# Cross-attention softmax on ScalarE from PSUM, and the first expert pair scaled by ScalarE

## The chip, the cores and the metric

One core of a Trainium2 chip runs one program. The metric is the device time in microseconds (us), the median of three runs. The engines are TensorE (PE, with its weight loads PEld), VectorE (DVE), ScalarE (ACT), GpSimd (POOL) and SyncE (SP), which issues the transfers. Each runs its own queue of instructions in order; semaphores tie them together. Matmul results land in PSUM banks; VectorE and ScalarE read them there and write to SBUF.

## What is computed

64 sequences of 256 tokens, 256 channels, in fp32. First a cross-attention block with a context of 77 rows and 8 heads of 64, then a block in which routing weights over 16 experts mix projections:

```python
x = x + xattn(layernorm(x), ctx)            # heads 8, width 64, context 77
    # q = x@Wq, k = ctx@Wk, v = ctx@Wv
    # softmax(q k^T * SCALE) v, then @Wo + bo         SCALE = 64 ** -0.5
x = x + ffn(layernorm(x))
    # rw = gating(x)                       weights over 16 experts, per token
    # q = sum_e rw[e] * (x @ q_proj[e]), likewise k and v   (64 columns each)
    # attn = causal softmax(q k^T / 8) v
    # out = sum_e (attn * rw[e]) @ o_proj[e]
```

## The kernel before, in words

A sequence has two tiles of 128 tokens. fp32 products are made of three products of a high and a low part (`_hi`, `_lo`, in a rounded format), by `product` (lines 371 to 375): so most PSUM results are copied by ScalarE into the high part and subtracted from it by VectorE into the low part.

The work of a sequence is cut into pieces with one function each on every engine that takes part: `a_...` is the cross-attention, `b_...` LayerNorm 2, routing and the expert projections, `c_...` the second attention and the output experts. Each engine runs `step(i)` for one sequence after the other: a list, written by hand, of pieces of sequence i+1 (`ahead`), i (`now`), i-1 (`before`) and i-2 (`earlier`). That list is the engine's order (TensorE lines 610 to 654, ScalarE 782 to 810, VectorE 1054 to 1105, GpSimd 1262 to 1279); a piece waits at its start for what it needs, and everything behind it in the same list waits with it.

PSUM has three rings of banks: `bank_a` (3), `bank_b` (3) and `bank_c` (2). Fill number f of a ring uses bank f modulo the ring's size, so TensorE may only start fill f when fill f-3 (in a and b) has been read. `ring_a` and `ring_b` (lines 380 to 393) wait for that. The fills that matter here: the four score blocks `a_s` 0 to 3 are fills 7 to 10 of ring a, the transposes `a_pT` 0 and 1 fills 11 and 12, `a_pv` 0 fill 13. So `a_s` 3 follows `a_s` 0 in the same bank, `a_pT` 0 and 1 follow `a_s` 1 and 2, and `a_pv` 0 follows `a_s` 3. The expert projections are `b_qkv` 0 to 15, two of the 16 experts for one token tile each; `b_qkv` j+3 follows `b_qkv` j in a bank of ring b. `b_qkv` 0 and 1 (the opening pair, one for each tile) also hold the routing logits.

A score block holds four heads for one token tile, 4 x 77 = 308 columns. VectorE takes the row maximum of each head from PSUM (line 923) and writes scores minus maximum to `probs` in SBUF (line 925), which frees the bank. ScalarE takes the exponential in place, one instruction of 308 columns, with the factor SCALE (line 719). VectorE sums the exponentials of two blocks (line 930) and takes the reciprocal (line 933), and GpSimd multiplies (line 1247). TensorE then transposes `probs` (line 485).

The routing weights `rw` come last from a chain: sum (line 977) and reciprocal (line 979) on VectorE, product on GpSimd (line 1224). VectorE scales the two experts of `b_qkv` 0 and 1 by `rw` into the accumulators `acc` (line 993) and adds the other seven pairs to them (line 996). Of the second attention, `c_pT` (split on ScalarE at line 740 and on VectorE at line 1002), `c_pv` (its result copied by ScalarE at line 768), and `c_mix` 0 to 3 (VectorE line 1037, ScalarE 772, GpSimd 1252) lie near the change. ScalarE's softmax there (`c_exp`, line 754) already uses a bias from SBUF and an accumulator.

Of the kernel before, what the change touches and what calls it, by code (L numbers as in the profile page):

```python
# [34 lines left out]
def xattn_moe_kernel(nc, x, ctx_in, Wq, Wk, Wv, Wo, bo, sim_matrix, gates, q_proj, k_proj, v_proj, o_proj, out, rw_dram):  # L35
# [35 lines left out]
    def b_at(n, fill):  # L71
        return B_FILLS * n + fill + 1
# [2 lines left out]
        return C_FILLS * n + fill + 1  # L75

    def a_read(n, fill):
        assert fill % A_FILLS != A_K
        return (A_FILLS - 1) * n + fill + (1 if fill < A_K else 0)

    def b_read(n, fill):
        return (B_QKV + 2 * NT * EP) * n + (fill + 1 if fill < B_QKV else 2 * fill)

    C_READ = {C_QK: 0, C_S: 2, C_PT: 3, C_Y: 4}

# [19 lines left out]
    with es:  # L105
# [6 lines left out]
        def sem(name):  # L112
            return es.enter_context(nc.semaphore(name))
# [256 lines left out]
        def _(pe):  # L370
# [9 lines left out]
            def ring_a(n, fill):  # L380
                if fill - A_BANKS == A_K:
                    pe.wait_ge(k_ready, at(1, n, 0))
                elif fill >= A_BANKS:
                    pe.wait_ge(a_evac, a_read(n, fill - A_BANKS))
                elif not (known(n) and n == 0):
                    pe.wait_ge(a_evac, a_read(n - 1, fill - A_BANKS + A_FILLS))

            def ring_b(n, fill):
                if not (known(n) and n == 0 and fill < B_BANKS):
                    if fill >= B_BANKS:  # L390
# [212 lines left out]
            def step(i):  # L603
                ahead, now, before, earlier = i + 1, i, i - 1, i - 2

                def do(n, fn, *k):
                    if on(n):
                        fn(n, *k)

                do(before, b_qkv, 6)  # L610
                do(before, b_qkv, 7)
                do(earlier, c_y, 0)
                do(before, b_qkv, 8)
                do(earlier, c_y, 1)
# [24 lines left out]
                do(now, b_qkv, 0)  # L639
                do(now, b_qkv, 1)  # L640
                do(ahead, a_kT)
                do(before, c_s)
                do(ahead, a_q, 0)
                do(ahead, a_q, 1)
                do(now, b_qkv, 2)
                do(ahead, a_s, 0)
                do(before, c_pT)
                do(ahead, a_s, 1)
                do(ahead, a_s, 2)
                do(ahead, a_s, 3)  # L650
                do(before, c_pv)
                do(now, b_qkv, 3)
                do(now, b_qkv, 4)
                do(now, b_qkv, 5)
# [10 lines left out]
        def _(act):  # L665
# [6 lines left out]
            def split_weights(k):  # L672
                hi = PIECES[k][1]
                act.wait_ge(wt_in[k % SLOTS], 16 * loads_before(k))
                nc.scalar.activation(hi, stage[k % SLOTS][:, 0:hi.shape[1]], copy).then_inc(wt_hi, 1)

            for k in range(EARLY):
                split_weights(k)
# [36 lines left out]

            def a_exp(n, j):
                half, t = j // 2, j % 2
                act.wait_ge(a_evac, a_read(n, A_S + j))
                nc.scalar.activation(probs[:, t, half * HB:(half + 1) * HB, :], probs[:, t, half * HB:(half + 1) * HB, :],  # L719
                                     ACT.Exp, scale=SCALE).then_inc(p_exp, 1)  # L720

            def a_pT(n, j):
                t = j % 2
# [10 lines left out]
            def b_exp(n):  # L734
                act.wait_ge(g_ready, at(1, n, 0))
                nc.scalar.activation(w[:, :, :], g[:, :, :], ACT.Exp).then_inc(e_ready, 1)

            def c_part(n, fill, dst, src):
                act.wait_ge(c_fill, c_at(n, fill))
# [34 lines left out]
            def step(i):  # L774
                ahead, now, before, earlier = i + 1, i, i - 1, i - 2

                def do(n, fn, *k):
                    if on(n):
                        fn(n, *k)
                        later(split_weights, fn.__name__.replace("exp", "s"), n, *k)  # L780
# [22 lines left out]
                do(ahead, a_q, 1)  # L803
                do(now, b_exp)
                do(before, c_pT)
                do(before, c_pv)
                do(before, c_mix, 0)
                do(ahead, a_exp, 0)
                do(before, c_mix, 1)
                do(before, c_mix, 2)  # L810

# [9 lines left out]
        def _(dve):  # L821
# [12 lines left out]
            def split_weights(k):  # L834
                dve.wait_ge(wt_hi, k + 1)
                for lo, hi, rows, cols in PIECES[k][2]:
                    last = V.tensor_tensor(lo, stage[k % SLOTS][rows, cols], hi.bitcast(F32), ALU.subtract)
                last.then_inc(wt_ready, 1)

            def ln_a(k, n, src):  # L840
# [76 lines left out]
                last.then_inc(a_evac, 1)  # L917

            def a_s(n, j):
                half, t = j // 2, j % 2  # L920
# [60 lines left out]
            def b_qkv(n, j):  # L981
                fill, ep, t = B_QKV + j, j // NT, j % NT
                dve.wait_ge(b_fill, b_at(n, fill))
                if j == 0:
                    dve.wait_ge(rw_ready, at(1, n, 0))
                if ep == 0 and not (known(n) and n == 0):
                    dve.wait_ge(qkv_ready, at(NT, n - 1, t))
                for k in range(2):
                    e = 2 * ep + k
                    lo = (E if ep == 0 else 0) + k * QKV  # L990
                    src = bank_b(fill)[:, lo:lo + QKV]
                    if ep == 0:
                        V.tensor_scalar(acc[:, t, k, :], src, rw[:, t, e:e + 1], None, ALU.mult).then_inc(b_evac, 1)  # L993
                    else:
                        dve.wait_ge(b_evac, b_read(n, fill - NT) - 1 + k)
                        V.scalar_tensor_tensor(acc[:, t, k, :], src, rw[:, t, e:e + 1], acc[:, t, k, :],  # L996
                                               ALU.mult, ALU.add).then_inc(b_evac, 1)


            def c_part(n, fill, which, pair, src):  # L1000
# [45 lines left out]
            def step(i):  # L1046
# [96 lines left out]
        def _(pool):  # L1143
# [98 lines left out]
                G.tensor_tensor(v2[1][:, :, :, :], v_in, v2[0].bitcast(F32)[:, :, :, :], ALU.subtract).then_inc(v2_ready, 1)  # L1242

            def a_p(n, half):
                pool.wait_ge(p_sum_ready, at(4, n, 2 * half + 1))
# [72 lines left out]
```

## Time and profile before

| | us |
|---|---|
| median of three runs (2802.65 to 2807.08) | 2802.98 |
| the profiled run's own time | 2805.71 |
| its span, from first to last instruction | 2803.8 |
| TensorE matmuls busy | 2702.4 (96%) |
| VectorE busy | 2439.1 (87%) |
| ScalarE busy | 1020.0 (36%) |
| GpSimd busy | 1190.0 (42%) |
| mean granted TensorE clock | 0.991 of full |

The busy shares say which engine is nearly full. They don't say where it waits: for that there are the table of waits (who waited for whom, summed), the timeline (instructions with their start in us from the span's start, their duration, and idle time before them in brackets) and the busy time in a window. In the steady part the steps repeat with the same times, so one step can be read for all.

### The profile page before, as it was taken

To read this page: it belongs to the slowest core of one execution; us is meant where nothing else is said; L and a number is where in the kernel's file an instruction comes from. 1 tells how busy PE (TensorE), PEld (TensorE's weight loads), DVE (VectorE), ACT (ScalarE), POOL (GpSimd) and SP (SyncE) were. 2 spreads that over 40 slices of the span, in tenths; PEclk is the share of its full clock that TensorE was granted. 3 is DMA by queue.
4 is the path that set the end of the run, shared out by engine and by line. 5 is a ranking of instruction groups with operands and counts; after the bars stand their busy time and mean duration, and the time that the engine had idled before them with its cause. 6 is when DMAs were issued, how large, how long until landed. Compare 5 with 4: busy or idle time off the path is not lost.

```text
span 2803.8 us, 64494 instructions
## 1 busy us (share of the span) xinstructions
PE 2702.4 (96%) x19012; PEld 2581.8 (92%) x19012; DVE 2439.1 (87%) x6755; ACT 1020.0 (36%) x2448; POOL 1190.0 (42%) x1739
## 2 busy tenths in 40 slices
PE   5999999999999999999999999999999999999996
PEld 4999999999999999999999999999999999999996
DVE  6898888888888888988988889888889889888884
ACT  3343333333333333433333333333334334333331
POOL 1343443444444434434434434444344344344343
PEclk8999999999999999999999999999999999999998
DMA  4111111111111111111111111111111111111111
GB/s 103 29 45 44 32 44 35 40 44 28 44 48 28 44 44 31 44 44 31 44 39 36 44 30 41 48 28 44 44 31 44 44 31 44 43 32 44 35 36 39
DMA packets 131435, 113.58 MB, mean 41 GB/s; under 512 B 24720, under 2 KB 130640, under 8 KB 131408
## 3 DMA queue, kind: packets, MB, share of 16 engines
q1 hardware_dynamic: 131408, 113.23, 16.5%
q8 instruction: 15, 0.25, 0.0%
q14 instruction: 12, 0.10, 0.0%
HBM read 95.38 MB, written 17.83 MB: 40 GB/s over the span
## 4 chain that ended last, share of the span: by engine, by line
PE 73%; DVE 12%; issue 9%; ACT 4%; POOL 1%; DVEq 1%; POOLq 0%; DMA 0%; ACTq 0%; SPq 0%
PE bank_b L373 9%; PE bank_b L374 8%; PE bank_a L375 8%; PE bank_b L375 8%; PE bank_a L374 8%; PE bank_a L373 8%; PE bank_c L373 4%; PE bank_c L375 4%; PE bank_c L374 4%; PE bank_a L485 4%; DVE acc L996 3%; DVE acc L993 2%; DVE mix L1037 1%; PE bank_a L445 1%; DVE s_max L923 1%
## 5 line engine op out<-in xcount | busy, mean ns | idle before, releaser
L373 PE MATMUL bank_b<-wqkv_hi,x2T_lo 128*128 128x384 f32 (+1 forms) x2048 | 726.4, 355 | 34.3 <-DVE acc L996 33.7
L374 PE MATMUL bank_b<-wqkv_lo,x2T_hi 128*128 128x384 f32 (+1 forms) x2048 | 693.5, 339 | 0.0
L375 PE MATMUL bank_b<-wqkv_hi,x2T_hi 128*128 128x384 f32 (+1 forms) x2048 | 688.8, 336 | 0.0
L996 DVE SCALAR_TENSOR_TENSOR acc<-bank_b,rw,acc 128x192 f32<-128x192 f32 x1792 | 641.6, 407 | 5.3 <-PE bank_b L375 2.9
L1252 POOL TENSOR_TENSOR mixs_lo<-mix,mixs_hi 128x512 fp32r<-128x512 f32 x256 | 379.9, 1514 | 153.7 <-ACT mixs_hi L772 153.7
L373 PEld LDWEIGHTS bank_b<-wqkv_hi,x2T_lo 128*128 128x128 f32 x2048 | 385.8, 188 | 57.5 <-DVE acc L996 53.6
L374 PEld LDWEIGHTS bank_b<-wqkv_lo,x2T_hi 128*128 128x128 f32 x2048 | 386.2, 189 | 0.0
L375 PEld LDWEIGHTS bank_b<-wqkv_hi,x2T_hi 128*128 128x128 f32 x2048 | 385.1, 188 | 0.0
L1174 POOL TENSOR_TENSOR pow_out<-pow_in,expo 128x2 f32<-128x2 f32 (+1 forms) x128 | 111.7, 873 | 596.4 <-DVE pow_in L853 509.3
L373 PE MATMUL bank_c<-wo_hi,mixs_lo 128*128 128x256 f32 x1024 | 293.9, 287 | 3.7 <-POOL mixs_lo L1252 3.7
L375 PE MATMUL bank_c<-wo_hi,mixs_hi 128*128 128x256 f32 x1024 | 288.0, 281 | 0.0
L374 PE MATMUL bank_c<-wo_lo,mixs_hi 128*128 128x256 f32 x1024 | 287.9, 281 | 0.0
L1037 DVE TENSOR_TENSOR mix<-rw_all,aT 128x512 f32<-128x512 f32 x256 | 243.0, 970 | 2.3 <-ACT aT L768 2.1
L772 ACT ACTIVATE mixs_hi<-mix 128x512 fp32r<-128x512 f32 x256 | 160.6, 628 | 205.6 <-DVE mix L1037 205.6
L1247 POOL TENSOR_TENSOR probs<-probs,p_sum 128x616 f32<-128x616 f32 x128 | 155.9, 1218 | 175.7 <-DVE p_sum L933 175.7
L682 ACT ACTIVATE aT_hi<-bank_a 128x512 fp32r<-128x512 f32 x128 | 76.4, 597 | 412.8 <-PE bank_a L375 412.8
L373 PEld LDWEIGHTS bank_c<-wo_hi,mixs_lo 128*128 128x128 f32 x1024 | 193.6, 189 | 4.1 <-issue 3.8
L374 PEld LDWEIGHTS bank_c<-wo_lo,mixs_hi 128*128 128x128 f32 x1024 | 194.4, 190 | 0.0
L375 PEld LDWEIGHTS bank_c<-wo_hi,mixs_hi 128*128 128x128 f32 x1024 | 193.9, 189 | 0.0
L889 DVE TENSOR_TENSOR aT_lo<-bank_a,aT_hi 128x512 fp32r<-128x512 f32 x128 | 88.5, 692 | 116.7 <-ACT aT_hi L682 116.7
L719 ACT ACTIVATE probs<-probs 128x308 f32<-128x308 f32 x256 | 117.2, 458 | 185.4 <-DVE probs L925 185.4
L889 DVE TENSOR_TENSOR pT_lo<-bank_a,pT_hi 77x512 fp32r<-77x512 f32 x256 | 162.9, 676 | 0.2 <-ACT pT_hi L682 0.2
(196 smaller groups left out, 6991.1 us busy)
## 6 DMA issues: line engine op xcount, KB each, us to landing
rw_all<-rw_dram SPq DMA_DIRECT2D x128, 512.0 KB, 5.7
xt<-in_x_dram SPq DMA_DIRECT2D x64, 256.0 KB, 2.7
out_dram<-mix SPq DMA_DIRECT2D x64, 256.0 KB, 2.2
ct<-in_ctx_dram SPq DMA_DIRECT2D x64, 57.8 KB
ct<-in_ctx_dram SPq DMA_DIRECT2D x64, 19.2 KB
mix<-in_L_ffn_o_proj_dram SPq DMA_DIRECT2D x2, 512.0 KB, 4.2
rw_dram<-rwT SPq DMA_DIRECT2D x64, 16.0 KB, 1.4
x_tiles<-in_L_xattn_Wq_dram SPq DMA_DIRECT2D x1, 512.0 KB, 6.9
```

Source lines behind the costliest of these rows:

```text
L373: nc.tensor.matmul(dst, lhs[1], rhs[0], start=start, stop=False)
L374: nc.tensor.matmul(dst, lhs[0], rhs[1], start=False, stop=False)
L375: return nc.tensor.matmul(dst, lhs[0], rhs[0], start=False, stop=stop)
L485: last = nc.tensor.transpose(bank_a(fill)[0:NC, k * P:(k + 1) * P], probs[:, t, half * HB + k, :], ident[:, :])
L719: nc.scalar.activation(probs[:, t, half * HB:(half + 1) * HB, :], probs[:, t, half * HB:(half + 1) * HB, :], ACT.Exp, scale=SCALE).then_in ...
L772: nc.scalar.activation(mixs[0][:, 2 * j:2 * j + 2, :], mix[:, 2 * j:2 * j + 2, :], copy).then_inc(mix_hi, 1)
L889: V.tensor_tensor(pair[1], src, pair[0].bitcast(F32), ALU.subtract).then_inc(a_evac, 1)
L996: V.scalar_tensor_tensor(acc[:, t, k, :], src, rw[:, t, e:e + 1], acc[:, t, k, :], ALU.mult, ALU.add).then_inc(b_evac, 1)
L1037: V.tensor_tensor(mix[:, 2 * j:2 * j + 2, :], rw_all[:, 2 * j:2 * j + 2, :], aT2[:, :].unsqueeze(1).to_broadcast([P, 2, T]), ALU.mult).the ...
L1174: G.tensor_tensor(dst, src, expo[:, 0:m], ALU.pow).then_inc(ln_pow[k], 1)
L1247: G.tensor_tensor(part, part, p_sum[:, half, 1, :, :].unsqueeze(3).to_broadcast([P, NT, HB, NC]), ALU.mult).then_inc(p_ready, 1)
L1252: G.tensor_tensor(mixs[1][:, 2 * j:2 * j + 2, :], mix[:, 2 * j:2 * j + 2, :], mixs[0].bitcast(F32)[:, 2 * j:2 * j + 2, :], ALU.subtract).t ...
```

## The change

The exponentials of the cross-attention are taken from PSUM by ScalarE: for each head an instruction of 77 columns, with the negated maximum as bias and the row's sum as accumulator output. VectorE's subtraction and its sum go; it keeps the maximum (negated in the same instruction) and the reciprocal, which now waits for the exponentials. SCALE moves into Wq when the weights are split at the start. A score bank is now free when its exponentials are done: the fills that follow (`a_s` 3, `a_pT` 0 and 1, `a_pv` 0) wait for `p_exp`.

The opening expert pair is scaled by ScalarE (`b_first`, two copies of 192 columns with a scale from SBUF for each tile), signalled by `acc_first`; `b_qkv` 3 and 4 on TensorE and `b_qkv` 2 and 3 on VectorE wait for it. In ScalarE's order the two `b_first` come after `c_pT`, and `a_exp` 0 now comes after them and ahead of `c_pv` and `c_mix` 0. In TensorE's order `c_pv` moves ahead of `a_s` 3.

```diff
@@ TensorE, ring_a and ring_b @@
+                elif A_S <= fill - A_BANKS < A_S + 2 * NT:
+                    pe.wait_ge(p_exp, at(2 * NT, n, fill - A_BANKS - A_S))
...
+                    if B_QKV <= fill - B_BANKS < B_QKV + NT:
+                        pe.wait_ge(acc_first, at(NT, n, fill - B_BANKS - B_QKV))
@@ TensorE, step @@
                 do(ahead, a_s, 2)
+                do(before, c_pv)
                 do(ahead, a_s, 3)
-                do(before, c_pv)
@@ ScalarE @@
-                nc.scalar.activation(hi, stage[k % SLOTS][:, 0:hi.shape[1]], copy).then_inc(wt_hi, 1)
+                nc.scalar.activation(hi, stage[k % SLOTS][:, 0:hi.shape[1]], copy,
+                                     scale=SCALE if k == W_Q else 1.0).then_inc(wt_hi, 1)
...
             def a_exp(n, j):
                 half, t = j // 2, j % 2
-                act.wait_ge(a_evac, a_read(n, A_S + j))
-                nc.scalar.activation(probs[:, t, half * HB:(half + 1) * HB, :], probs[:, t, half * HB:(half + 1) * HB, :],
-                                     ACT.Exp, scale=SCALE).then_inc(p_exp, 1)
+                act.wait_ge(s_max_ready, at(2 * NT, n, j))
+                for k in range(HB):
+                    last = nc.scalar.activation(probs[:, t, half * HB + k, :], bank_a(A_S + j)[:, k * NCE:k * NCE + NC], ACT.Exp,
+                                                bias=s_max[:, j, k:k + 1], accum_out=p_sum[:, half, 0, t, k:k + 1])
+                last.then_inc(p_exp, 1)
...
+            def b_first(n, t):
+                act.wait_ge(rw_ready, at(1, n, 0))
+                act.wait_ge(b_fill, b_at(n, B_QKV + t))
+                if known(n) and n == 0:
+                    act.wait_ge(sim_step, 5)
+                else:
+                    act.wait_ge(qkv_ready, at(NT, n - 1, t))
+                for e in range(2):
+                    last = nc.scalar.activation(acc[:, t, e, :], bank_b(B_QKV + t)[:, E + e * QKV:E + (e + 1) * QKV], copy,
+                                                scale=rw[:, t, e:e + 1])
+                last.then_inc(acc_first, 1)
@@ ScalarE, step @@
                 do(before, c_pT)
+                do(now, b_first, 0)
+                do(now, b_first, 1)
+                do(ahead, a_exp, 0)
                 do(before, c_pv)
                 do(before, c_mix, 0)
-                do(ahead, a_exp, 0)
@@ VectorE @@
             def a_s(n, j):
...
-                V.tensor_reduce(s_max[:, j, :], src, AX.X, ALU.max).then_inc(s_max_ready, 1)
-                dve.wait_ge(s_max_ready, at(2 * NT, n, j))
-                V.tensor_tensor(probs[:, t, half * HB:(half + 1) * HB, :], src,
-                                s_max[:, j, :].unsqueeze(2).to_broadcast([P, HB, NC]), ALU.subtract).then_inc(a_evac, 1)
+                V.tensor_reduce(s_max[:, j, :], src, AX.X, ALU.max, negate=True).then_inc(s_max_ready, 1)
             def a_psum(n, half):
                 dve.wait_ge(p_exp, at(2 * NT, n, 2 * half + 1))
-                V.tensor_reduce(p_sum[:, half, 0, :, :], probs[:, :, half * HB:(half + 1) * HB, :], AX.X,
-                                ALU.add).then_inc(p_sum_ready, 1)
-                dve.wait_ge(p_sum_ready, at(4, n, 2 * half))
+                if not (known(n) and n == 0):
+                    dve.wait_ge(p_ready, at(2, n - 1, half))
                 V.reciprocal(p_sum[:, half, 1, :, :], p_sum[:, half, 0, :, :]).then_inc(p_sum_ready, 1)
...
-                    if ep == 0:
-                        V.tensor_scalar(acc[:, t, k, :], src, rw[:, t, e:e + 1], None, ALU.mult).then_inc(b_evac, 1)
+                    if ep == 1:
+                        dve.wait_ge(acc_first, at(NT, n, t))
@@ VectorE, step @@
                 do(before, c_pT)
-                do(now, b_qkv, 0)
-                do(now, b_qkv, 1)
                 do(now, b_qkv, 2)
```

Besides, VectorE's split of Wq multiplies by SCALE, the counts in `a_read` and `b_read` follow, and GpSimd's `a_p` waits for the new count of the reciprocals.

## Rows read from the trace of the kernel before

**Rows 1.** The page: busy time; chain that ended last; line 719's group.
```profile
PE 2702.4 (96%) x19012; PEld 2581.8 (92%) x19012; DVE 2439.1 (87%) x6755; ACT 1020.0 (36%) x2448; POOL 1190.0 (42%) x1739
...
PE 73%; DVE 12%; issue 9%; ACT 4%; POOL 1%; DVEq 1%; POOLq 0%; DMA 0%; ACTq 0%; SPq 0%
...
L719 ACT ACTIVATE probs<-probs 128x308 f32<-128x308 f32 x256 | 117.2, 458 | 185.4 <-DVE probs L925 185.4
```

**Rows 2.** Windows, one step: length; busy PE, PEld, DVE, ACT, POOL; clock, DMA.
```profile
1340.73:1383.32 42.59, 41.88 (x298) 40.10 (x297) 37.78 (x106) 15.72 (x38) 18.54 (x27) 1.00 0.16 39
```

**Rows 3.** Waits of TensorE's weight loads, whole run: us in total, times, longest.
```profile
PEld bank_b L373 <- DVE acc L996: 53.6, 62, 0.9
PEld bank_c L541 <- POOL late_tiles L1232: 26.7, 60, 0.5
PEld bank_c L549 <- DVE k_stack L1007: 18.3, 59, 0.3
```

**Rows 4.** Timeline of TensorE at `b_qkv` 7: start, duration, instruction, idle before.
```profile
1353.48 0.33 PE L375 MATMUL bank_b<-wqkv_hi,x2T_hi 128*128 128x384 f32 x1
1354.37 0.44 PE L373 MATMUL bank_b<-wqkv_hi,x2T_lo 128*128 128x384 f32 x1 [0.55 <-DVE acc L996]
1354.65 0.34 PE L374 MATMUL bank_b<-wqkv_lo,x2T_hi 128*128 128x384 f32 x1
```

**Rows 5.** Timeline of VectorE in the same step, `a_s` 0 to `b_qkv` 4.
```profile
1346.63 0.48 DVE L923 TENSOR_REDUCE s_max<-bank_a 128x4 f32<-128x308 f32 x1 [0.26 <-PE bank_a L375]
1347.14 0.48 DVE L925 TENSOR_TENSOR probs<-bank_a,s_max 128x308 f32<-128x308 f32 x1
1347.54 0.17 DVE L977 TENSOR_REDUCE w_sum<-w 128x2 f32<-128x32 f32 x1
1347.75 0.17 DVE L979 RECIPROCAL w_sum<-w_sum 128x2 f32<-128x2 f32 x1
...
1348.42 1.39 DVE L993 TENSOR_SCALAR acc<-bank_b,rw 128x192 f32<-128x192 f32 x4
1349.73 0.73 DVE L996 SCALAR_TENSOR_TENSOR acc<-bank_b,rw,acc 128x192 f32<-128x192 f32 x2
1350.38 1.28 DVE L1037 TENSOR_TENSOR mix<-rw_all,aT 128x512 f32<-128x512 f32 x2
...
1352.23 1.42 DVE L1037 TENSOR_TENSOR mix<-rw_all,aT 128x512 f32<-128x512 f32 x1
1353.58 0.73 DVE L996 SCALAR_TENSOR_TENSOR acc<-bank_b,rw,acc 128x192 f32<-128x192 f32 x2
```

**Rows 6.** Groups by line, VectorE, one step: count, busy us, mean ns.
```profile
L930 DVE TENSOR_REDUCE p_sum<-probs 128x8 f32<-128x616 f32 x2 | 1.6, 782 | 0.0
```

**Rows 7.** Timeline of ScalarE: the second attention's softmax, then `c_pT`.
```profile
1344.01 0.39 ACT L754 ACTIVATE late_tiles<-late_tiles,m 128x128 f32<-128x128 f32 x1
1344.30 0.19 ACT L754 ACTIVATION_READ_ACCUMULATOR late_tiles<-late_tiles,m 128x1 f32 x1
1344.39 0.50 ACT L754 ACTIVATE late_tiles<-late_tiles,m 128x256 f32<-128x256 f32 x1
...
1346.97 0.49 ACT L740 ACTIVATE p2T_hi<-bank_c 128x384 fp32r<-128x384 f32 x1 [1.30 <-PE bank_c L557]
```

**Rows 8.** Timeline of ScalarE: copies of 77 columns from PSUM.
```profile
1375.39 0.24 ACT L692 ACTIVATE cT_hi<-bank_a 128x77 fp32r<-128x77 f32 x1 [5.56 <-PE bank_a L424]
1375.52 0.22 ACT L693 ACTIVATE cT_hi<-bank_a 64x77 fp32r<-64x77 f32 x1
```

**Rows 9.** Timeline of GpSimd: the routing weights.
```profile
1348.08 0.24 POOL L1224 TENSOR_TENSOR rw<-w,w_sum 128x32 f32<-128x32 f32 x1 [1.10 <-DVE w_sum L979]
```

**Rows 10.** Timeline of TensorE: first matmuls of `a_s` 3, `c_pv` and `b_qkv` 3.
```profile
1348.07 0.28 PE L373 MATMUL bank_a<-kT_hi,qT_lo 128*128 128x156 f32 x1
...
1348.74 0.32 PE L373 MATMUL bank_c<-p2T_hi,v_lo 128*128 128x256 f32 x1
...
1349.41 0.39 PE L373 MATMUL bank_b<-wqkv_hi,x2T_lo 128*128 128x384 f32 x1
```

More of the change, by code:

```diff
@@ L77, in a_read @@
     def a_read(n, fill):
-        assert fill % A_FILLS != A_K
-        return (A_FILLS - 1) * n + fill + (1 if fill < A_K else 0)
+        assert fill != A_K and not A_S <= fill < A_S + 2 * NT
+        return (A_FILLS - 1 - 2 * NT) * n + fill + (1 if fill < A_K else 0) - (2 * NT if fill > A_S else 0)
     def b_read(n, fill):
-        return (B_QKV + 2 * NT * EP) * n + (fill + 1 if fill < B_QKV else 2 * fill)
+        assert not B_QKV <= fill < B_QKV + NT
+        return (B_QKV + 2 * NT * (EP - 1)) * n + (fill + 1 if fill < B_QKV else 2 * (fill - NT))
     C_READ = {C_QK: 0, C_S: 2, C_PT: 3, C_Y: 4}
@@ L229, in xattn_moe_kernel @@
         pad_done = sem("pad_done")
+        acc_first = sem("acc_first")
         passed = sem("passed")
@@ L389, in ring_b @@
                 if not (known(n) and n == 0 and fill < B_BANKS):
-                    if fill >= B_BANKS:
+                    if B_QKV <= fill - B_BANKS < B_QKV + NT:
+                        pe.wait_ge(acc_first, at(NT, n, fill - B_BANKS - B_QKV))
+                    elif fill >= B_BANKS:
                         pe.wait_ge(b_evac, b_read(n, fill - B_BANKS))
@@ L836, in split_weights @@
                 for lo, hi, rows, cols in PIECES[k][2]:
-                    last = V.tensor_tensor(lo, stage[k % SLOTS][rows, cols], hi.bitcast(F32), ALU.subtract)
+                    if k == W_Q:
+                        last = V.scalar_tensor_tensor(lo, stage[k % SLOTS][rows, cols], SCALE, hi.bitcast(F32),
+                                                      ALU.mult, ALU.subtract)
+                    else:
+                        last = V.tensor_tensor(lo, stage[k % SLOTS][rows, cols], hi.bitcast(F32), ALU.subtract)
                 last.then_inc(wt_ready, 1)
@@ L919, in a_s @@
             def a_s(n, j):
-                half, t = j // 2, j % 2
                 src = bank_a(A_S + j)[:, 0:HB * NCE].rearrange("p (a b) -> p a b", a=HB)[:, :, 0:NC]
                 dve.wait_ge(a_fill, a_at(n, A_S + j))
-                V.tensor_reduce(s_max[:, j, :], src, AX.X, ALU.max).then_inc(s_max_ready, 1)
-                dve.wait_ge(s_max_ready, at(2 * NT, n, j))
-                V.tensor_tensor(probs[:, t, half * HB:(half + 1) * HB, :], src,
-                                s_max[:, j, :].unsqueeze(2).to_broadcast([P, HB, NC]), ALU.subtract).then_inc(a_evac, 1)
+                V.tensor_reduce(s_max[:, j, :], src, AX.X, ALU.max, negate=True).then_inc(s_max_ready, 1)
             def a_psum(n, half):
                 dve.wait_ge(p_exp, at(2 * NT, n, 2 * half + 1))
-                V.tensor_reduce(p_sum[:, half, 0, :, :], probs[:, :, half * HB:(half + 1) * HB, :], AX.X,
-                                ALU.add).then_inc(p_sum_ready, 1)
-                dve.wait_ge(p_sum_ready, at(4, n, 2 * half))
+                if not (known(n) and n == 0):
+                    dve.wait_ge(p_ready, at(2, n - 1, half))
                 V.reciprocal(p_sum[:, half, 1, :, :], p_sum[:, half, 0, :, :]).then_inc(p_sum_ready, 1)
@@ L983, in b_qkv @@
                 dve.wait_ge(b_fill, b_at(n, fill))
[L984 to L987, printed above, removed]
                 for k in range(2):
                     e = 2 * ep + k
-                    lo = (E if ep == 0 else 0) + k * QKV
-                    src = bank_b(fill)[:, lo:lo + QKV]
-                    if ep == 0:
-                        V.tensor_scalar(acc[:, t, k, :], src, rw[:, t, e:e + 1], None, ALU.mult).then_inc(b_evac, 1)
+                    src = bank_b(fill)[:, k * QKV:(k + 1) * QKV]
+                    if ep == 1:
+                        dve.wait_ge(acc_first, at(NT, n, t))
                     else:
                         dve.wait_ge(b_evac, b_read(n, fill - NT) - 1 + k)
-                        V.scalar_tensor_tensor(acc[:, t, k, :], src, rw[:, t, e:e + 1], acc[:, t, k, :],
-                                               ALU.mult, ALU.add).then_inc(b_evac, 1)
+                    V.scalar_tensor_tensor(acc[:, t, k, :], src, rw[:, t, e:e + 1], acc[:, t, k, :],
+                                           ALU.mult, ALU.add).then_inc(b_evac, 1)
             def c_part(n, fill, which, pair, src):
@@ L1244, in a_p @@
             def a_p(n, half):
-                pool.wait_ge(p_sum_ready, at(4, n, 2 * half + 1))
+                pool.wait_ge(p_sum_ready, at(2, n, half))
                 part = probs[:, :, half * HB:(half + 1) * HB, :]
```

## The prediction

> **What bounds the kernel now.** I read the page first: TensorE is busy 96% of the span, VectorE 87%, ScalarE 36%, and TensorE holds 73% of the chain that ended last [rows 1]. VectorE's 12% of that chain shows that it sometimes hands TensorE its work late. The profiled run took 2805.71 us (span 2803.8), 2.7 us above the median of the three times, 2802.98; my sum starts at 2805.71, and I take 2.7 off at its end.
>
> The kernel repeats one step for each of 64 sequences. A stretch of one step lasts 42.59 us, with 41.88 us of matmuls, 37.78 us of VectorE and 15.72 us of ScalarE [rows 2]. So a lighter VectorE as such gives nothing; only the places where TensorE stands still count. The table of waits names three that come back in nearly every step [rows 3]: the weight load of an expert projection waits for VectorE's accumulation at line 996 (53.6 us, 62 times), the transposes of query and key wait for GpSimd's sum (26.7 us, 60 times), and the scores of the second attention wait for `k_stack` (18.3 us, 59 times).
>
> The first is the one that the change is near. In the timeline the matmuls of `b_qkv` 6 run 0.17 to 0.18 us apart; the next one, the first of `b_qkv` 7, should start at 1353.65, starts at 1354.37, and the second follows 0.28 later instead of 0.175. The loss is 0.72 + 0.10 = 0.82 us a step [rows 4]. Its cause is the bank of `b_qkv` 4, which VectorE reads only from 1353.58 on, since it is behind: from 1346.63 it works without a gap [rows 5].
>
> **VectorE, what is removed.** In each step four subtractions at line 925 (0.48 us each), four scalings at line 993 (1.39 us together) [rows 5] and two sums at line 930 (0.782 us each) [rows 6] go: 1.9 + 1.4 + 1.6 = 4.9 us of 37.78. Before the stalling read lie one subtraction, 0.50 us from start to start, and the scalings, 1.31 us (1348.42 to 1349.73) [rows 5]. That is 1.8 us ahead of a delay of 0.82, so by itself the stall at `b_qkv` 7 goes: minus 0.82 us in 62 steps, minus 51 us. The other two stalls stay: the path from the output projection over LayerNorm, `b_qkv` 15 and GpSimd's sum, and the one over ScalarE's four copies into `k_stack`, hold nothing that is removed. Negating the maximum costs nothing (the same reduction); scaling Wq's low part happens once, beside the start's DMAs, within 1 us either way. The reciprocal now waits for the exponentials instead of a sum; its old partner is gone.
>
> **ScalarE, what is added.** Of the exponentials, one of 308 columns (0.458 us) [rows 1] becomes four of 77, each with a read of the accumulator behind it. The nearest rows are those of the second attention's softmax [rows 7]: with a bias from SBUF and an accumulator the 128-column one takes 0.39, its read begins 0.29 after it and the next exponential 0.09 after that. The 256-column one takes 0.50, so a column costs about 0.8 ns and 51 columns fewer take off 0.04: 0.35 for 77 columns, a read 0.25 after it, and a pair each 0.34. Four pairs to the end of the last read (0.19) are 3 x 0.34 + 0.25 + 0.19 = 1.46 us. These rows read SBUF where the new ones read PSUM, so I keep both ends: 1.23 (a pair at 0.28, as if most of the read were hidden), and 2.16 if exponential (0.35) and read (0.19) don't overlap at all. ScalarE gets about 4 x 1.0 = 4 us a step more, plus the scalings; of 42.59 it now uses 15.7, so it doesn't become the bound by load.
>
> The opening pair's scalings are four copies of 192 columns from PSUM with a scale from SBUF. A plain copy of 77 columns from PSUM takes 0.24, and the next starts 0.13 after it, so 0.1 overlaps [rows 8]; with 0.8 ns a column 192 take 0.33 and start 0.23 apart. The exponential with a bias from SBUF and an accumulator is 0.11 longer than a plain copy of 128 columns would be (0.39 against 0.28). If the operand from SBUF is the reason, the scalings take 0.44 and start 0.34 apart. I take 0.34, since the row with such an operand is the nearest; 0.23 and 0.44 (no overlap) are the ends. The rows don't say whether the 0.11 belongs to the operand or to the accumulator. The Trainium skill does ("ScalarE: Activation LUTs", section "What ACT_TABLE_LOAD costs"): a per-partition pointer operand adds about 93 ns to an ACTIVATE and neighbours overlap by about the same; by its formula the four would be an estimated 4 x 0.346 = 1.38 us against my 1.36, where without that rule the low end, 0.92, would be as good.
>
> **The new wait, and who stands behind it.** Score block `a_s` 3 uses the bank of `a_s` 0. Until now it waited for VectorE's subtraction, over at 1347.62, and its matmuls ran from 1348.07: no stall. Now it waits for ScalarE's exponentials of block 0, and those are queued behind the two `b_first`, which wait for the routing weights. I follow it in the times of this step:
> - VectorE's maximum starts at 1346.63. Without the subtraction the sum of weights starts at 1347.04 instead of 1347.54, its reciprocal at 1347.25 instead of 1347.75, and GpSimd's `rw`, at 1348.08 now, 0.50 earlier, at 1347.58 [rows 5, 9].
> - The first user of `rw` starts 0.34 after it (1348.42 now) [rows 5, 9], so `b_first` starts at 1347.92. ScalarE is free by then (its copy of p2T ends at 1347.46) [rows 7].
> - Four scalings, 1.36: 1349.28. Four exponentials, 1.46: 1350.74. A weight load follows its release by 0.06 (accumulation over at 1354.31, matmul at 1354.37) [rows 4, 5]: 1350.80.
> - TensorE has work until then from the second attention's `c_pv`, which the change puts ahead of `a_s` 3. It would start at 1348.07 and be done after 0.67 (1348.74 to 1349.41 now) [rows 10]: 1348.74. VectorE's c_pT part is then ready at about 1348.05, just in time.
>
> So TensorE stands 1350.80 - 1348.74 = 2.06 us, and 0.05 for the slow first matmul: 2.11 us in each of 63 steps (all sequences but the first), plus 133 us.
>
> **What is queued behind it.** On TensorE the `b_qkv` 3 to 7; on ScalarE `c_pv`, then VectorE's `c_mix` and GpSimd's four `mixs_lo`. All start from the same event, so they move together. From the release of `a_s` 3, `b_qkv` 7 is due after 0.7 + 4 x 1.05 = 4.9 us (a projection is six matmuls by 0.175). VectorE's read of `b_qkv` 4 ends 4.6 to 4.8 after it: two `c_mix` end at about 1.6 (0.4 of ScalarE's copy and 1.28), `b_qkv` 3 can be read from 1.9 on and takes 0.65, then 1.35 for a `c_mix` beside GpSimd (1352.23 to 1353.58) and 0.73 [rows 5]. The cover is only 0.1 to 0.3 us; if it is gone, up to 0.3 us a step comes back (19 us). Further on blocks 1 to 3 have 1.46 each where 0.46 was; the transposes of `a_pT` and `a_pv` 0 keep by the same bookkeeping some 0.5 to 0.7 us of cover.
>
> **Sum.** 2805.7 + 133 - 51 = 2888 in the profiled run's terms, 2885 against the median. With the low ends of both ScalarE costs (0.92 + 1.23 instead of 2.82) the wait is 1.44 and the sum 63 x 0.67 = 42 us less, 2843; without overlap (1.76 + 2.16) it is 3.21 and the sum 69 more, 2954. Start and end of the run, some 80 us outside the steady steps, I leave as they are, within 5 us.
>
> **Rivals.**
> - *Slower still: ScalarE's chain becomes a second wait.* Small instructions don't overlap; `a_s` 3 costs 3.2 us, and the three later blocks are 0.7 us longer each, 2.1 us against some 0.7 of cover before `a_pv` 0, which costs another 1.4 a step. That is 2954 to 3040. Against it: the read of the accumulator overlaps both its neighbours by 0.1 [rows 7]. Chance 12%.
> - *The stall at `b_qkv` 7 survives in part,* because `c_mix` now starts after the exponentials. 0.3 us a step: 2904. For it: the cover of 0.1 to 0.3. Chance 13%.
> - *Faster: ScalarE's leg is short.* From the release of `rw` to the last exponential I have 2.82 us. If it is below 1.5 the new wait is smaller than the 0.82 that goes. At 1.3 the wait is 0.54 + 0.05, the step 0.23 shorter, 2789 us. It would need the scalings 0.15 and the exponentials 0.18 apart; the only pair so close is the 77-column copy at 0.13, without accumulator [rows 8]. Chance 6%.
> - *About even,* a leg near 1.5: 3%.
>
> **How the numbers follow.** The forecast (2843 to 2920) has 66%, the surviving stall 13%, the second wait 12%, even 3%, faster 6%. I name 2885. The range is 2835 to 2945: it leaves out the two last and most of the second wait. A measurement tells about 0.2% from no change. Faster 6%, within 0.2% 3%, slower 91%.
>
> **What would show it.** In the changed profile: a wait of the weight load at line 373 in bank_a for ScalarE's `probs`, about 2 us, 63 times; none, or under 0.3 us, of `b_qkv` 7 for VectorE; VectorE's busy time near 2439 - 64 x 4.9 = 2125 us; ScalarE's near 1020 + 64 x 5.4 = 1366; the other two waits as now; pairs of exponential and read 0.34 apart; scalings 0.34 apart; the step 43.9 us. I am wrong if ScalarE's leg is well under 2.4 us, or if a wait that I don't list, before `a_pT` or `a_pv` 0, appears.

## The result and the profile after

The changed kernel is slower: 2949.39 us, median of four runs (2947.88 to 2949.59), against 2803.93 for the kernel before in the same comparison. The ratio is 1.0516, with a 95% interval from 1.0498 to 1.0534. I had named 2885 us with 2945 as the upper end. The direction was right, the size was not: 64 of the 145 us were missing from the sum.

The page of the kernel after, busy time, chain and the group of the new exponentials (line 727; every row has the line numbers of its own kernel, so line 375 here is line 373 of the kernel before):

```profile
PE 2776.1 (94%) x19012; PEld 2668.4 (91%) x19012; DVE 2122.6 (72%) x6115; ACT 1313.3 (45%) x4496; POOL 1162.7 (39%) x1739
...
PE 82%; ACT 9%; DVE 4%; issue 3%; POOL 1%; ACTq 0%; DMA 0%; POOLq 0%; DVEq 0%; SPq 0%
...
L727 ACT ACTIVATE probs<-bank_a,s_max 128x77 f32<-128x77 f32 x1024 | 317.2, 335 | 57.5 <-DVE s_max L949 57.5
```

VectorE is 316 us less busy than in [rows 1], and ScalarE's share of the chain went from 4% to 9%. But TensorE has 74 us more of busy time with the same 19012 matmuls: some of them ran longer. The same can be seen in the mean granted clock, 0.962 against 0.991 before.

The waits of TensorE's weight loads, whole run:

```profile
PEld bank_a L375 <- ACT probs L727: 113.2, 64, 2.7
PEld bank_c L547 <- POOL late_tiles L1247: 26.9, 60, 0.5
PEld bank_c L555 <- DVE k_stack L1024: 19.1, 59, 0.3
```

The first line is the new wait of `a_s` 3, 113.2 / 64 = 1.77 us in the mean. The wait for VectorE's accumulation that headed [rows 3] (53.6 us) is gone, and the other two are as they were.

What stands behind the new wait is in TensorE's timeline: the end of `c_pv`, the first matmuls of `a_s` 3, and `b_qkv` 3 to 5.

```profile
1328.36 0.28 PE L377 MATMUL bank_c<-p2T_hi,v_hi 128*128 128x128 f32 x1
1330.27 0.34 PE L375 MATMUL bank_a<-kT_hi,qT_lo 128*128 128x156 f32 x1 [1.63 <-ACT probs L727]
1330.45 0.28 PE L376 MATMUL bank_a<-kT_lo,qT_hi 128*128 128x156 f32 x1
...
1331.22 0.52 PE L376 MATMUL bank_b<-wqkv_lo,x2T_hi 128*128 128x384 f32 x1
1331.54 0.52 PE L377 MATMUL bank_b<-wqkv_hi,x2T_hi 128*128 128x384 f32 x1
...
1334.69 0.34 PE L375 MATMUL bank_b<-wqkv_hi,x2T_lo 128*128 128x384 f32 x1
1334.87 0.34 PE L376 MATMUL bank_b<-wqkv_lo,x2T_hi 128*128 128x384 f32 x1
```

TensorE stood from the end of `c_pv` to 1330.27. One us after it resumed, the projections are 0.32 us apart instead of 0.175. Eleven of them take 3.47 us (1331.22 to 1334.69) instead of 1.93: 1.55 us lost. The windows of these stretches (columns as in [rows 2]; the clock is the third number from the end) show the clock:

```profile
1328.00:1330.20 2.20, 0.64 (x6) 0.50 (x5) 0.74 (x2) 2.20 (x13) 0.69 (x1) 1.00 0.12 13
1330.20:1332.00 1.80, 1.73 (x10) 1.73 (x11) 1.29 (x2) 0.97 (x4) 0.00 (x0) 0.78 0.39 129
1332.00:1334.00 2.00, 2.00 (x8) 2.00 (x7) 0.94 (x3) 0.55 (x1) 1.97 (x2) 0.50 0.00 0
1334.00:1336.00 2.00, 2.00 (x11) 2.00 (x11) 2.00 (x4) 0.63 (x1) 0.71 (x2) 0.84 0.00 0
1336.00:1338.00 2.00, 2.00 (x14) 2.00 (x13) 1.38 (x4) 1.62 (x8) 2.00 (x2) 1.00 0.00 0
```

The granted clock is full up to the stand, falls to 0.50 (1.2 of 2.4 GHz) behind it and is back at 1.00 by 1336; 0.78 and 0.84 are windows in which it changes. By the Trainium skill ("TensorE: Matmul & The Clock Gate", section "What's actually happening") the clock has two states, full and half, and how busy TensorE has been lately decides between them. The windows agree with the two states, 1.00 and 0.50; whether the stand is the reason, the experiments have to show.

Not every step has it. At 611.77 `a_s` 3 stood for the same time, and the projections behind it run at full pace:

```profile
611.77 0.34 PE L375 MATMUL bank_a<-kT_hi,qT_lo 128*128 128x156 f32 x1 [1.63 <-ACT probs L727]
...
612.90 0.33 PE L377 MATMUL bank_b<-wqkv_hi,x2T_hi 128*128 128x384 f32 x1
613.07 0.33 PE L375 MATMUL bank_b<-wqkv_hi,x2T_lo 128*128 128x384 f32 x1
```

The windows from one start of `a_s` 3 to the next tell three kinds of step apart (the last row is a stretch behind the start at 744.27):

```profile
611.77:655.41 43.64, 41.83 (x297) 40.22 (x297) 33.06 (x95) 20.31 (x71) 18.45 (x27) 1.00 0.15 38
655.41:700.61 45.20, 43.38 (x297) 41.77 (x297) 32.38 (x95) 20.29 (x71) 17.94 (x27) 0.96 0.14 37
744.27:790.96 46.69, 44.91 (x298) 43.30 (x298) 33.01 (x95) 20.30 (x71) 17.64 (x27) 0.93 0.14 36
...
744.20:750.80 6.60, 6.53 (x22) 6.53 (x23) 3.54 (x8) 2.16 (x5) 3.35 (x3) 0.50 0.10 35
```

Of the 49 steps that start between 400 and 2600 us, 17 are of the first kind (43.64 us, full clock), 24 of the second (45.21 us, one fall of 3.4 us) and 8 of the third (46.70 us, a fall of 6.8 us). So two steps in three have a fall, and the falls cost (24 x 1.57 + 8 x 3.06) / 49 = 1.27 us a step.

The account of a step without a fall: the stand costs 1.80 us (from 1328.47, where `a_s` 3 would have followed, to 1330.27) and 0.07 for the slow first matmul, and the old stall's 0.82 is gone. That makes 1.05 us more, and 43.64 is 1.05 above the 42.59 of [rows 2]. Over the whole run, start and end included, the spans differ by (2946.1 - 2803.8) / 63 = 2.26 us a step, which leaves 1.21 us for the clock.

That the stand makes the clock fall was theory (A) for the experiments. Its rival (B) was that the projections behind `a_s` 3 are slow because ScalarE, VectorE and GpSimd start on the same event and use the memories beside them. The steps at full pace, such as the one from 611.77, have the same work beside them and already speak against it. A third question was which half of the change, or which place in an order, makes the stand.

### The profile page after: what moved, and what is told of

It is laid out like the page before. It is cut to its first block, busy times and chain, and to the rows that moved or that the text cites. A ratio compares the mean times of both kernels' runs of the same rounds, so it can differ in the third digit from the quotient of the medians.

```text
span 2946.1 us, 65793 instructions
## 1 busy us (share of the span) xinstructions
PE 2776.1 (94%) x19012; PEld 2668.4 (91%) x19012; DVE 2122.6 (72%) x6115; ACT 1313.3 (45%) x4496; POOL 1162.7 (39%) x1739
## 4 chain that ended last, share of the span: by engine, by line
PE 82%; ACT 9%; DVE 4%; issue 3%; POOL 1%; ACTq 0%; DMA 0%; POOLq 0%; DVEq 0%; SPq 0%
PE bank_b L375 12%; PE bank_b L376 11%; PE bank_b L377 11%; PE bank_a L375 9%; PE bank_a L377 8%; PE bank_a L376 8%; PE bank_c L375 4%; PE bank_c L377 4%; PE bank_c L376 4%; PE bank_a L491 4%; ACT probs L727 3%; ACT acc L755 2%; PE bank_a L451 1%; DVE s_max L949 1%; PE bank_c L555 1%
## 5 line engine op out<-in xcount | busy, mean ns | idle before, releaser
L376 PE MATMUL bank_b<-wqkv_lo,x2T_hi 128*128 128x384 f32 (+1 forms) x2048 | 716.7, 350 | 0.0
L377 PE MATMUL bank_b<-wqkv_hi,x2T_hi 128*128 128x384 f32 (+1 forms) x2048 | 711.7, 348 | 0.0
L1267 POOL TENSOR_TENSOR mixs_lo<-mix,mixs_hi 128x512 fp32r<-128x512 f32 x256 | 357.1, 1419 | 286.7 <-ACT mixs_hi L793 286.7
L375 PEld LDWEIGHTS bank_b<-wqkv_hi,x2T_lo 128*128 128x128 f32 x2048 | 408.5, 199 | 0.2
L376 PEld LDWEIGHTS bank_b<-wqkv_lo,x2T_hi 128*128 128x128 f32 x2048 | 405.6, 198 | 0.0
L727 ACT ACTIVATE probs<-bank_a,s_max 128x77 f32<-128x77 f32 x1024 | 317.2, 335 | 57.5 <-DVE s_max L949 57.5
L1054 DVE TENSOR_TENSOR mix<-rw_all,aT 128x512 f32<-128x512 f32 x256 | 198.2, 796 | 87.9 <-ACT aT L789 87.9
L375 PE MATMUL bank_a<-kT_hi,qT_lo 128*128 128x156 f32 x512 | 153.8, 300 | 104.5 <-ACT probs L727 104.2
L727 ACT ACTIVATION_READ_ACCUMULATOR probs<-bank_a,s_max 128x1 f32 x1024 | 222.7, 217 | 0.0
L375 PEld LDWEIGHTS bank_a<-kT_hi,qT_lo 128*128 128x128 f32 x512 | 104.5, 204 | 113.7 <-ACT probs L727 113.2
```

The lines of the kernel that those rows point to most:

```text
L375: nc.tensor.matmul(dst, lhs[1], rhs[0], start=start, stop=False)
L376: nc.tensor.matmul(dst, lhs[0], rhs[1], start=False, stop=False)
L377: return nc.tensor.matmul(dst, lhs[0], rhs[0], start=False, stop=stop)
L727: last = nc.scalar.activation(probs[:, t, half * HB + k, :], bank_a(A_S + j)[:, k * NCE:k * NCE + NC], ACT.Exp, bias=s_max[:, j, k:k + 1], ...
L1054: V.tensor_tensor(mix[:, 2 * j:2 * j + 2, :], rw_all[:, 2 * j:2 * j + 2, :], aT2[:, :].unsqueeze(1).to_broadcast([P, 2, T]), ALU.mult).the ...
L1267: G.tensor_tensor(mixs[1][:, 2 * j:2 * j + 2, :], mix[:, 2 * j:2 * j + 2, :], mixs[0].bitcast(F32)[:, 2 * j:2 * j + 2, :], ALU.subtract).t ...
```

## The experiments

Each is compared with the kernel before, timed beside it (medians 2804.98 to 2806.03 us).

**Filling the stand with matmuls that nobody reads.**

```diff
+            def filler(n):
+                for k in range(12):
+                    nc.tensor.matmul(bank_c(C_PT)[:, 0:C], wo[0][:, 0, 0:P], wo[0][:, 0, :],
+                                     start=True, stop=True)
...
                 do(before, c_pv)
+                do(before, filler)
                 do(ahead, a_s, 3)
```

> The changed kernel with 12 extra matmuls of 256 columns (their result is never read) between c_pv and a_s 3, in the time in which TensorE waits for the exponentials of block 0. Theory A (the clock): the wait of about 1.8 us in each step makes the granted clock fall to half for some us behind it, and this costs about 1.2 us a step on average; twelve matmuls by 0.12 us fill 1.44 us of the wait, the clock stays full, a_s 3 starts when it did: 2949 - 63 x 1.2 = about 2872 us. Theory B (the matmuls behind the wait are slow since ScalarE, VectorE and GpSimd use the memories at the same time): no change, 2949 us, and those matmuls stay 0.32 us apart.

Measured: 2873.96 us, ratio 1.0245 (1.0228 to 1.0262). More work and 75 us less time. In three fences: its waits in a stretch of 2200 us of the steady part (the one used for all waits below), its timeline, and the window of that stretch:

```profile
PEld bank_a L375 <- ACT probs L733: 17.7, 50, 0.4
```

```profile
1338.75 1.64 PE L568 MATMUL bank_c<-wo_hi 128*128 128x256 f32 x12
1340.54 0.34 PE L375 MATMUL bank_a<-kT_hi,qT_lo 128*128 128x156 f32 x1
1340.71 0.28 PE L376 MATMUL bank_a<-kT_lo,qT_hi 128*128 128x156 f32 x1
```

```profile
400.00:2600.00 2200.00, 2182.83 (x15567) 2097.92 (x15567) 1667.60 (x4800) 1021.74 (x3518) 927.78 (x1361) 1.00 0.16 38
```

`a_s` 3 waits for the same exponentials and starts no earlier: 1340.54 is 2.53 us after `c_pv`'s first matmul at 1338.01, and 1375.48 is 2.53 after 1372.95 in the kernel after. Only the clock differs, 1.00 in the window where the kernel after has 0.97, and ScalarE and the others do the same work beside the projections. Theory B falls. Over the whole run the clock costs (2946.1 - 2871.7) / 63 = 1.18 us a step.

**A shorter filler: 5 matmuls instead of 12.**

```diff
-                for k in range(12):
+                for k in range(5):
```

> The changed kernel with 5 extra matmuls instead of the 12 of the filler run: TensorE stands idle for about 1.2 us instead of 1.8 (without filler) or 0.4 (with 12). The start of a_s 3 isn't moved. If the clock only falls after a stand as long as 1.8 us, this is 2874 us, as with 12; if 1.2 us is already too long, it is near 2949.

Measured: 2872.82 us, ratio 1.0239 (1.0222 to 1.0256), the same as with 12. TensorE now stands for a good microsecond in each step (waits, then timeline),

```profile
PEld bank_a L375 <- ACT probs L733: 59.3, 50, 1.2
```

```profile
1338.53 0.81 PE L568 MATMUL bank_c<-wo_hi 128*128 128x256 f32 x5
1340.31 0.34 PE L375 MATMUL bank_a<-kT_hi,qT_lo 128*128 128x156 f32 x1 [0.97 <-ACT probs L733]
```

and pays nothing for it in clock: all 50 steps between 400 and 2600 us last 43.6 us, as the steps without a fall do in the kernel after. In this kernel a stand of 1.2 us is free of it and one of 1.8 is not.

**Real work in the stand: `b_qkv` 3 ahead of `a_s` 3.**

```diff
                 do(before, c_pv)
-                do(ahead, a_s, 3)
                 do(now, b_qkv, 3)
+                do(ahead, a_s, 3)
                 do(now, b_qkv, 4)
```

> The changed kernel with b_qkv 3 ahead of a_s 3 in TensorE's order: 1.05 us of real work in the wait, so 0.8 us of it is left, as long as the stall of the kernel before. Theory A (the clock): the wait is 1.05 shorter and the clock stays full, 2949 - 63 x (1.05 + 1.2) = about 2807 us. Theory B (contention): 2949 - 66 = 2883 us.

Measured: 2836.02 us, ratio 1.011 (1.0093 to 1.0126): 113 us less than the kernel after, far more than the 66 of theory B, but 29 us above what A had expected. The waits in the same 2200 us say why:

```profile
PEld bank_a L375 <- ACT probs L727: 42.8, 51, 0.8
PEld bank_b L375 <- DVE acc L1013: 27.7, 51, 0.6
```

The stand of `a_s` 3 is down to 0.84 us, as expected, and the mean clock is 0.99. But the stall at a projection that waits for VectorE is back with 0.54 us: TensorE reaches it 1.05 us earlier, VectorE doesn't, since its `c_mix` still starts from ScalarE's copy of `c_pv`. In 62 steps that is 33 us; the difference to the expectation is 29.

**The exponentials of block 0 ahead of the scalings on ScalarE.**

```diff
-                do(now, b_first, 0)
-                do(now, b_first, 1)
                 do(ahead, a_exp, 0)
+                do(now, b_first, 0)
+                do(now, b_first, 1)
                 do(before, c_pv)
```

> The changed kernel with a_exp 0 ahead of the two b_first in ScalarE's order. The exponentials of block 0 need only VectorE's maximum, over 0.7 us before rw, and take 1.2 us: they end before c_pv does, a_s 3 doesn't wait and the clock stays full. The stall at b_qkv 7 is gone too if VectorE keeps ahead. Theory A: 2804 - 51 = about 2753 us. Rival: the scalings come 1.2 us later and with them c_pv's copy and c_mix, so part of the stall at b_qkv 7 comes back (0.3 us a step), 2770 us; if the order of the two doesn't matter, 2949.

Measured: 2797.21 us, ratio 0.9969 (0.9958 to 0.9981). The wait of `a_s` 3 is gone and with it all of the loss: the same instructions as in the kernel after, in another order, are 152 us faster. But it is 44 us above the expectation. Again there is a row of waits for VectorE, and VectorE's timeline says why:

```profile
PEld bank_b L375 <- DVE acc L1013: 35.9, 52, 0.7
...
1348.10 0.74 DVE L1013 SCALAR_TENSOR_TENSOR acc<-bank_b,rw,acc 128x192 f32<-128x192 f32 x2 [1.37 <-ACT acc L755]
```

0.69 us a step at the projections, in a kernel in which VectorE has 4.9 us less to do. It stands 1.37 us ahead of `b_qkv` 2 for the scalings, which are now behind the exponentials on ScalarE, and from there to its read of `b_qkv` 4 it works almost without a gap.

**ScalarE's copy of `c_pv` between the scalings,** to see whether the copy holds `b_qkv` 7 (against the order of the last experiment).

```diff
                 do(ahead, a_exp, 0)
                 do(now, b_first, 0)
-                do(now, b_first, 1)
                 do(before, c_pv)
+                do(now, b_first, 1)
```

> Both halves of the change, with another order on ScalarE: a_exp 0, b_first 0, the copy of c_pv, b_first 1. In the run with only a_exp 0 put ahead (2797 us) a stall of 0.7 us a step at b_qkv 7 stayed. If it stays because c_mix 0 waits for c_pv's copy, which stands behind both scalings, the copy now comes 0.6 us earlier, c_mix and with it b_qkv 4 too, and the stall falls to about 0.1: 2797 - 63 x 0.6 = 2760 us. Rival (VectorE's load or the late accumulators hold b_qkv 7, not the copy): within 5 us of 2797.

Measured: 2778.7 us, ratio 0.9909 (0.9892 to 0.9925). The stall falls, but only from 0.69 to 0.44 us:

```profile
PEld bank_b L375 <- DVE acc L1013: 23.1, 52, 0.5
```

The median went down by 18.5 us, (0.69 - 0.44) x 63 = 16 of them here. The rival (within 5 us of 2797) is refuted and the copy is part of the cause; my 0.6 us was too much. VectorE still stands 1.36 us for the scalings ahead of `b_qkv` 2, by the trace; no run tests what would take that wait away.

**Each half of the change alone.** First the exponentials, with the scalings back on VectorE:

```diff
# from the kernel after
-                do(now, b_first, 0)
-                do(now, b_first, 1)
                 do(ahead, a_exp, 0)
...
# VectorE
                 do(before, c_pT)
+                do(now, b_qkv, 0)
+                do(now, b_qkv, 1)
                 do(now, b_qkv, 2)
```

> Only the softmax half of the change: the exponentials on ScalarE from PSUM, the opening pair's scalings back on VectorE at their old place, the rest as in the changed kernel (c_pv ahead of a_s 3). Nothing stands before a_exp 0 on ScalarE, so a_s 3 waits for nothing or 0.1 us. VectorE reaches b_qkv 4 0.5 us earlier than before the change, since a subtraction is gone from that stretch; the stall there falls from 0.8 to 0.3 us: 2804 - 63 x 0.5 = about 2772 us. Rival (the exponentials themselves cost the time, wherever the scalings are): 2850 or more.

Measured: 2771.99 us, ratio 0.9878 (0.9861 to 0.9894), as expected to the microsecond. TensorE waits for VectorE's accumulation 0.29 us a step:

```profile
PEld bank_b L374 <- DVE acc L1013: 14.9, 52, 0.3
```

Then the scalings alone, from the kernel before:

```diff
# ScalarE, from the kernel before
                 do(before, c_pT)
+                do(now, b_first, 0)
+                do(now, b_first, 1)
                 do(before, c_pv)
# VectorE
-                do(now, b_qkv, 0)
-                do(now, b_qkv, 1)
                 do(now, b_qkv, 2)
```

> The kernel before with only the scaling half of the change: the opening pair scaled by ScalarE, ahead of c_pv's copy; the exponentials and TensorE's order as before. No score bank waits for ScalarE, so a_s 3 doesn't wait and the clock stays full. VectorE loses 1.3 us ahead of b_qkv 2, but waits for the first scaling (rw at 1348.3, two scalings, 1349.1), so it gains only about 0.6 us, and c_mix 0 starts when ScalarE's copy of c_pv lets it, about 0.3 earlier than before. The stall at b_qkv 7 falls from 0.8 to about 0.5 us: 2804 - 63 x 0.3 = 2785 us. Rival (ScalarE's scalings cost the time of the change): 2850 or more.

Measured: 2798.99 us, ratio 0.9972 (0.9962 to 0.9982), with 0.74 us of stall left instead of 0.87. The gain is a third of what I had expected (6 us of 20). So neither half is slow: minus 33 us and minus 6 us alone, plus 145 together. The loss is in the order in which ScalarE does them, as the exponentials put ahead have shown.

**`c_pv` behind `a_s` 3 again,** the third part of the change undone in the kernel after.

```diff
                 do(ahead, a_s, 2)
-                do(before, c_pv)
                 do(ahead, a_s, 3)
+                do(before, c_pv)
```

> The changed kernel with c_pv behind a_s 3 again, as it was before. a_s 3 starts when ScalarE is done with block 0, as in the changed kernel, so TensorE stands 0.67 us longer, 2.5 us, and c_pv's 0.67 us follow it. c_pv's copy and c_mix come about 1.5 us later, so a part of the stall at b_qkv 7 may come back. By the move alone 2949 + 63 x 0.67 = 2991 us, with the stall up to 3030; the clock falls as in the changed kernel. If the clock stays down longer for a longer stand, more.

Measured: 3007.83 us, ratio 1.073 (1.0707 to 1.0754). The stand is 2.55 us, the stall at `b_qkv` 7 shows in some steps:

```profile
PEld bank_a L375 <- ACT probs L727: 122.6, 48, 2.6
...
PEld bank_b L375 <- DVE acc L1013: 7.7, 13, 0.6
```

The move of `c_pv` is worth 58 us to the kernel after, within what I had expected (2991 to 3030). The longer stand doesn't cost more clock (0.962 again). Of 48 steps 35 have a fall, and the 13 stalls of the second row are in exactly the 13 that have none: where the projections run at half the clock, VectorE has read the bank by the time that TensorE wants it. My "if the clock stays down longer for a longer stand, more" didn't come.

**The old stall without ScalarE: two lines of VectorE's order exchanged,** in the kernel before and in the one with the exponentials alone.

```diff
-                do(before, c_mix, 2)
                 do(now, b_qkv, 4)
+                do(before, c_mix, 2)
                 do(before, c_mix, 3)
```

> The kernel before, with two lines of VectorE's order exchanged: b_qkv 4 ahead of c_mix 2. If the stall at b_qkv 7 is only a matter of when VectorE reads b_qkv 4, it goes without any work moved to ScalarE: b_qkv 4 is read from 1352.3 on instead of 1353.6, minus 0.8 us a step: 2804 - 51 = 2753 us. Rival (VectorE is behind by its load, the stall moves to another projection or to c_y, whose low parts come 0.7 us later): 2780 to 2804.

Measured: 2807.27 us, ratio 1.0007 (0.9998 to 1.0017): no gain. The rival holds. The wait is as long as before, one projection further on (waits, VectorE's timeline, and that of the weight loads):

```profile
PEld bank_b L373 <- DVE acc L996: 46.3, 52, 0.9
```

```profile
1317.08 0.47 DVE L923 TENSOR_REDUCE s_max<-bank_a 128x4 f32<-128x308 f32 x1
1317.58 0.48 DVE L925 TENSOR_TENSOR probs<-bank_a,s_max 128x308 f32<-128x308 f32 x1
1317.98 0.73 DVE L996 SCALAR_TENSOR_TENSOR acc<-bank_b,rw,acc 128x192 f32<-128x192 f32 x2
```

```profile
1318.76 0.19 PEld L373 LDWEIGHTS bank_b<-wqkv_hi,x2T_lo 128*128 128x128 f32 x1 [0.89 <-DVE acc L996]
```

`b_qkv` 8 waits for the read of `b_qkv` 5 (1317.98), which stands behind all of `c_mix` and `a_s` 1. VectorE is behind by its load in this stretch, and exchanging two of its reads only moves the wait.

> The softmax half of the change (2772 us, 0.3 us of stall at b_qkv 7 left) with the same exchange, b_qkv 4 ahead of c_mix 2 on VectorE. The remaining 0.3 us goes: 2772 - 63 x 0.29 = 2754 us. If b_qkv 4's matmuls are not done when VectorE comes to it, it waits for them and c_mix 2 and 3 come later: 2760.

Measured: 2768.16 us, ratio 0.9859 (0.9839 to 0.9879). The stall of 0.29 us is gone from the projections and back before the transposes, with GpSimd as its releaser:

```profile
PEld bank_a L488 <- POOL probs L1264: 14.1, 50, 0.3
```

`c_mix` 2 came later, so GpSimd's `mixs_lo` and behind them its scaling of `probs` came later: 6.34 us from the first `mixs_lo` to `probs` (1335.25 to 1341.59) instead of 5.91 (1337.96 to 1343.87). 2768 against 2772 can't be told apart by these intervals. Both beat the kernel before by 1.2 to 1.4%, and the kernel after by 6%.

## Why the prediction was right or wrong

*The stall that was to go.* The number is right, minus 0.82 us a step, but not the reason, "by itself the stall at `b_qkv` 7 goes". VectorE has less to do, but what it gains it waits away, first for ScalarE's scalings and then for ScalarE's copy of `c_pv`:

```profile
1373.69 0.74 DVE L1013 SCALAR_TENSOR_TENSOR acc<-bank_b,rw,acc 128x192 f32<-128x192 f32 x2 [0.79 <-ACT acc L755]
1375.80 1.29 DVE L1054 TENSOR_TENSOR mix<-rw_all,aT 128x512 f32<-128x512 f32 x2 [1.37 <-ACT aT L789]
```

The stall is gone because TensorE itself comes later, by its new stand. Where TensorE comes 1.05 us earlier and nothing is moved on the other engines (`b_qkv` 3 ahead), 0.54 us of the stall are back; with the exponentials ahead it is 0.69, and the halves of the change alone leave 0.29 and 0.74. So the minus 51 us came with the stand and not beside it; that the term fits is in part luck.

*The new wait, its place and its cause.* Right. In the kernel after, ScalarE's timeline between `rw` and the last exponential is

```profile
1371.82 0.49 ACT L761 ACTIVATE p2T_hi<-bank_c 128x384 fp32r<-128x384 f32 x1 [1.30 <-PE bank_c L563]
1372.85 1.35 ACT L755 ACTIVATE acc<-bank_b,rw 128x192 f32<-128x192 f32 x4 [0.54 <-POOL rw L1239]
1374.08 0.34 ACT L727 ACTIVATE probs<-bank_a,s_max 128x77 f32<-128x77 f32 x1
1374.28 0.23 ACT L727 ACTIVATION_READ_ACCUMULATOR probs<-bank_a,s_max 128x1 f32 x1
1374.38 0.35 ACT L727 ACTIVATE probs<-bank_a,s_max 128x77 f32<-128x77 f32 x1
...
1375.18 0.24 ACT L727 ACTIVATION_READ_ACCUMULATOR probs<-bank_a,s_max 128x1 f32 x1
```

and the group of the scalings between 400 and 2600 us (count, busy us, mean ns) is

```profile
L755 ACT ACTIVATE acc<-bank_b,rw 128x192 f32<-128x192 f32 x196 | 66.3, 421 | 26.8 <-POOL rw L1239 26.8
```

Four scalings took 1.23 us (1.36 forecast), four exponentials 1.34 (1.46): a pair starts 0.30 after the last, not 0.34. The leg is 2.57 instead of 2.82. A scaling lasts 0.42 us where a plain copy of 192 columns would be 0.33 by the prediction's estimate. No read of an accumulator is in it, so the extra 0.09 goes to the operand from SBUF, as far as that estimate holds. The rule of the Trainium skill named beside that step ("ScalarE: Activation LUTs", section "What ACT_TABLE_LOAD costs") agrees, with its 93 ns. The stand was 1.87 us with its slow matmul, not 2.11: the step of the sum was right in kind and 0.24 us (15 us of the sum) too large. VectorE's busy time is as forecast (2122.6 us, 2125 forecast), ScalarE's is 1313.3 against 1366. The low end of the four exponentials comes to 1.28 by its own spacing, not 1.23, which decides nothing.

*What is queued behind it, and the cover before `a_pT` and `a_pv` 0.* Right for the kernel after: no new row there. The thin cover of 0.1 to 0.3 us before `b_qkv` 7 held, at full clock too, since neither filler run has a row of that stall. That it is thin shows in the experiments: with TensorE earlier at `b_qkv` 7 a part of the stall was there (0.54, 0.69, 0.44, 0.29 us).

*The price of a stand.* Wrong, and this is the step that failed. The sum has TensorE's stand as the time it lasts "and 0.05 for the slow first matmul". The stand of 1.8 us has a second price, 1.18 us a step over the run, in the clock of the matmuls behind it. Without it my terms give 2804 + 63 x (1.87 - 0.82) = 2870 us, and the filler run measured 2874; with it, 2870 + 74 = 2944, against 2949. All rows from which I took prices had stands up to 0.9 us at full clock; the trace of before held nothing at 1.8 us in the steady part, and I didn't ask what its clock would do. The mean clock of 0.991 in the page should have been a question: the shortfall lies at the start and the end of the run, where TensorE does stand for longer (the clock is 0.86 in the first 100 us, 0.92 from 2650 us on and 1.00 between).

*The rivals.* The 12% rival (2954 to 3040) came near the measured time, but for another reason (no overlap on ScalarE), which is false. The surviving stall, 13%, isn't in the kernel after. The faster rival asked for a shorter leg; it was the order, not the leg, that could have made the change a gain, and I didn't weigh it.

## What to carry to other kernels

When work is moved to an idle engine, what counts is the queue that it joins: here the same instructions cost 145 us or gave 8, by whether the exponentials that free a bank stood behind the scalings that wait for the routing weights, or ahead. Price a stand of TensorE twice, by its length and by the clock of what follows, and take the second price from a row of that length, or leave the range open for it. And fill a stand with matmuls that do nothing to tell a clock effect from contention: here the kernel with more work was 75 us faster, which contention for the memories can't explain.

## What the runs showed of the hardware

- A stand of 1.8 us, behind some 40 us of dense matmuls, was followed by matmuls at 0.50 of the clock in 32 of 49 steps, for 3.4 us in 24 of them (the step 1.57 us longer) and for 6.8 us in 8 (3.06 us longer). Behind stands of 1.2 us (50 steps) and 0.84 us (51 steps) there was no fall. With stands of 2.55 us it was 35 steps of 48, and the same mean clock, 0.962. Why a given step has the fall or not, the runs don't show.
- The fall isn't always at the stand: at 1330.2 `a_s` 3 still runs at full pace and the clock falls 1 us later. In the next step, at 1375.48, the matmuls are slow from the first one on. The same stand at 611.77 has no fall at all.
- On ScalarE a read of the accumulator costs 0.09 to 0.10 us of the queue though it lasts 0.19 to 0.24, since it overlaps both neighbours; from PSUM a pair with a 77-column exponential takes 0.30 us.
